# A first attention with 48-row scores: two 32-bit parts, alternating row halves, scores issued beside transposed scores

## What is computed

```python
# x: (4, 256, 256); 16 heads of 16 columns
q = _split(lora_linear(x, Wq, bq, Bq, Aq))       # k and v likewise
scores = jnp.einsum('bhqd,bhkd->bhqk', q, k) * SCALE
attn = jax.nn.softmax(scores, axis=-1)
out = jnp.einsum('bhqk,bhkd->bhqd', attn, v)
return lora_linear(out, Wo, bo, Bo, Ao)          # added to x by the caller
# feed-forward block: s = 1 / mean(|w|) of each of three weight matrices
```

## Time and the profile before

| | us |
|---|---|
| median of 3 runs | 788.89 (788.40 to 789.37) |
| the profiled execution | 788.12, span 786.3, mean granted clock 0.941 |
| first attention, from the start to its last residual | 0 to 109.4 |
| its loop on PE | 48.39 to 87.14 |
| its tail on PE | 87.14 to about 108 |
| loop of the cross-attention on PE | some 600 to 650 |

### The profile page before, as it was taken

How to read it: one execution, slowest core, us unless ns; L and a number is a source line. 1 busy time by engine, 2 the same in 40 slices (tenths; PEclk the granted TensorE clock), 3 DMA queues, 4 the chain that set the end, 5 groups by cost and what they waited for, 6 DMA issues and landing times. The chain is left out here.

```text
span 786.3 us, 13300 instructions
## 1 busy us (share of the span) xinstructions
PE 689.4 (88%) x4778; PEld 449.3 (57%) x4778; DVE 561.0 (71%) x1085; ACT 432.5 (55%) x896; POOL 196.8 (25%) x296
## 2 busy tenths in 40 slices
PE   5999989999999999999847469999868888889997
PEld 3555567566666756666433244666623444368886
DVE  5578678686868768686669973566568999475665
ACT  4557743635536373553649666455356999633222
POOL 2413001303032130303224514131022111352450
PEclk9999998999999999999978789999957999959999
DMA  4725432212112120210132205230020334403201
GB/s 124 190 66 163 132 102 61 75 23 66 47 43 51 52 76 19 71 45 7 28 119 33 75 8 148 79 99 3 2 61 6 72 82 106 120 2 109 78 29 54
DMA packets 55698, 53.59 MB, mean 68 GB/s; under 512 B 15526, under 2 KB 46310, under 8 KB 55526
## 3 DMA queue, kind: packets, MB, share of 16 engines
q1 hardware_dynamic: 54718, 52.27, 24.4%
q10 hardware_dynamic: 916, 0.47, 0.2%
HBM read 26.84 MB, written 2.04 MB: 37 GB/s over the span
## 5 line engine op out<-in xcount | busy, mean ns | idle before, releaser
L427 DVE TENSOR_REDUCE a_nm<-ps 128x2 f32<-128x512 f32 (+1 forms) x112 | 75.3, 688 | 28.2 <-PE ps L723 19.4
L2511 DVE TENSOR_REDUCE x_nm<-ps 128x2 f32<-128x512 f32 x128 | 80.0, 684 | 14.0 <-PE ps L2658 11.0
L1533 PE MATMUL ps<-m_xp,m_mp 128*128 128x512 f32 x288 | 77.4, 406 | 0.2 <-DVE m_wr L1236 0.2
L2594 ACT ACTIVATE x_pt<-ps 128x1024 f32<-128x1024 f32 x64 | 63.9, 1023 | 7.6 <-PE ps L2689 7.4
L1408 ACT ACTIVATE m_junk<-ps,m_nm 128x256 bf16<-128x256 f32 x128 | 58.6, 484 | 12.5 <-DVE m_nm L1253 12.5
L1200 POOL TENSOR_SCALAR fw<-fw,finv 128x256 f32<-128x256 f32 x24 | 11.6, 482 | 212.5 <-PE ps L1612 212.5
L2658 PE MATMUL ps<-kx,a_qs 48*128 48x256 bf16 x256 | 44.9, 297 | 19.3 <-DVE x_nm L2511 11.4
L1533 PEld LDWEIGHTS ps<-m_xp,m_mp 128*128 128x128 f32 x288 | 52.2, 193 | 14.7 <-issue 4.8
L3110 PE MATMUL ps<-x_xp,x_wp 128*128 128x512 f32 x216 | 54.8, 405 | 0.0
L1216 DVE TENSOR_TENSOR m_qcs<-ps,mw_tab 64x512 f32<-64x512 f32 x64 | 44.1, 688 | 7.6 <-PE ps L1533 6.1
L1223 DVE TENSOR_TENSOR m_qcs<-ps,mw_tab 128x512 f32<-128x512 f32 x64 | 41.2, 685 | 7.5 <-PE ps L1533 7.2
(11 more groups left out here) (304 smaller groups left out, 1660.3 us busy)
## 6 DMA issues: line engine op xcount, KB each, us to landing
a_qs<-a_parts SPq DMA_DIRECT2D x48, 128.0 KB
a_ks<-a_parts SPq DMA_DIRECT2D x48, 128.0 KB
m_q<-m_qs SPq DMA_DIRECT2D x32, 128.0 KB
x_gb<-scr_g SPq DMA_DIRECT2D x8, 512.0 KB, 3.7
fw<-in_f_w SPq DMA_DIRECT2D x12, 256.0 KB
a_qs<-a_ks SPq DMA_DIRECT2D x46, 64.0 KB
mw_wq<-in_m_wq SPq DMA_DIRECT2D x8, 256.0 KB, 2.9
mw_wo<-in_m_wo SPq DMA_DIRECT2D x8, 256.0 KB, 2.9
```

The source lines that it names most:

```text
L427: dve.tensor_reduce(dst, src, AX.X, ALU.max, negate=True).then_inc(mx_done.sem, 1)
L1533: mm = pe.matmul(c.ps[:, QB_BANKS[k], :], mp[:, p % 2, w, dt, tile * P:(tile + 1) * P], xp[:, x, dt, half_cols(half)], start=((dt, w, x) = ...
L2511: dve.tensor_reduce(nm[:, n % ITEMS, QT * u:QT * u + QT], c.ps[:, score_bank(n, u), :].rearrange("p (t k) -> p t k", t=QT), AX.X, ALU.max, ...
L2594: act.activation(pt[:, n % 2, kt, :], c.ps[:, 2 + 2 * kt:4 + 2 * kt, :].rearrange("p b n -> p (b n)"), ACT.Exp, scale=SCALE).then_inc(exp_ ...
```

## The change

The first attention gets a function of its own, `first_attention`; the second keeps `attention_block`, and the rest of the program is the same.

- q and k are split into two 32-bit parts (`F32R`): ACT writes the high part, DVE the remainder, which is the second part. Three products of parts make 48 rows (50 with the maxima). Items 0 to 3 and 8 to 11 lie on partitions 0 to 49, items 4 to 7 and 12 to 15 on 64 to 113. POOL's low part and ACT's middle part are gone.
- SP sends six transfers of 256 KB for each of k = 0 and 1. For k = 2 and 3 each batch is sent apart, in six of 128 KB: the first batch early, the second when its slot has come free (`later_in`, waited for by `scores(10, 0)` and `scores(14, 0)`).
- The loop runs 11 times over `side_by_side` four times, `product` twice and `max_transpose`; LAG is 5 instead of 4, TLAG 4 instead of 3, and from item 5 on the scores have three banks. The tail has five products and four transposed scores instead of four and three. `outputs(n)` of the loop moves from DVE to ACT.
- The twelve weight loads are issued before the first send, and ACT's twelve sums stand between the parts in the head; the first of them waits for all twelve loads.
- POOL clears a second stretch of 32 partitions, and the first send waits for both.

```diff
+def first_attention(c, wqk_in, wvo, bias_io, first, scales, last_loads):
...
+    Q_TERMS, K_TERMS = (0, 0, 1), (0, 1, 0)
+    S_ROWS = len(Q_TERMS) * HD
+    T_ROWS = S_ROWS + 2
+    BASES = (0, 64)
...
+    LAG, TLAG = 5, 4
...
+    ORDER = ((0, 0), (0, 1), (1, 1), (1, 0))
...
+        parts = sb("parts", [P, 2, DT, 2, TOK], F32R)
...
+        def rows_of(tiles, n, first_row, last_row):
+            base = BASES[n // 4 % 2]
+            return by_slot(tiles, slice(base + first_row, base + last_row), slot(n))[:, n % 2, :, :]
...
+        def score_bank(n, u):
+            i = UNITS * n + u
+            return i % 2 if n < LAG else (0, 1, 7)[(i - UNITS * LAG) % 3]
...
+                def send_term(k, w, part, term, b):
+                    half, ot = ORDER[k]
+                    base = BASES[k % 2]
+                    rows = slice(base + term, base + S_ROWS, len(Q_TERMS))
+                    if k < 2:
+                        sp.dma_start((qr, kr)[w][0][rows], parts[:, w, ot, part, half_cols(half)].bitcast(F32))\
+                            .then_inc(part_in[k].sem, 16)
+                    else:
+                        q0 = half * BANK + b * SEQ
+                        sp.dma_start(by_slot((qr, kr)[w], rows, (2, 0)[b]), parts[:, w, ot, part, q0:q0 + SEQ].bitcast(F32))\
+                            .then_inc((later_in[k] if b else part_in[k]).sem, 16)
...
+                scales.loads(sp)
+                sp.wait_ge(cleared.sem, cleared.at(2))
+                send_all(0)
+                send_all(1)
+                send_all(2)
+                send_all(3)
+                max_rows_in(4)
+                sp.wait_ge(st_done.sem, st_done.at(2 * 2))
+                send(2, 0, 0, 1)
+                send(2, 1, 0, 1)
+                max_rows_in(5)
+                send(2, 0, 1, 1)
+                send(2, 1, 1, 1)
+                for n in range(6, 9):
+                    max_rows_in(n)
+                sp.wait_ge(st_done.sem, st_done.at(2 * 6))
+                max_rows_in(9)
+                send(3, 0, 0, 1)
+                max_rows_in(10)
+                send(3, 1, 0, 1)
+                max_rows_in(11)
+                send(3, 0, 1, 1)
+                send(3, 1, 1, 1)
+                for n in range(12, N):
+                    max_rows_in(n)
+                last_loads(sp)
...
+                for base in BASES:
+                    pool.memset(c.kflat[base + 32:base + 64, :].bitcast(F32), 1.0).then_inc(cleared.sem, 1)
+                pool.wait_ge(cleared.sem, cleared.at(2))
...
+                def remainder(g):
+                    w, ot, half = parts_of(g)
+                    dve.wait_ge(hi_done.sem, hi_done.at(g + 1))
+                    dve.scalar_tensor_tensor(parts[:, w, ot, 1, half_cols(half)], c.ps[:, 2 + g % 4, :],
+                                             bcol[:, w, ot:ot + 1], parts[:, w, ot, 0, half_cols(half)].bitcast(F32),
+                                             ALU.add, ALU.subtract).then_inc(lo_done.sem, 1)
...
+                def outputs(n):
+                    act.wait_ge(av_done.sem, av_done.at(n + 1))
+                    act.activation(outputs_of(place(n)[0])[:, place(n)[1], :], c.ps[:, 6, 0:SEQ], ACT.Copy)\
+                        .then_inc(out_done.sem, 1)
...
+                high(2)
+                sums(0, 1)
+                high(3)
+                sums(1, 5)
+                high(4)
+                sums(5, 7)
+                high(5)
+                sums(7, 8)
+                high(6)
+                sums(8, 9)
+                high(7)
+                sums(9, 11)
+                values(0)
+                sums(11, 12)
...
+                for n in range(N - LAG):
+                    exponentials(n + 1, 0)
+                    exponentials(n + 1, 1)
+                    max_rows(n + TLAG)
+                    outputs(n)
...
+                def may_score(n, u):
+                    if u == 0 and n % 4 == 0:
+                        pe.wait_ge(part_in[n // 4].sem, part_in[n // 4].at(16 * 6))
+                    if u == 0 and n in (10, 14):
+                        pe.wait_ge(later_in[n // 4].sem, later_in[n // 4].at(16 * 6))
+                    i = UNITS * n + u
+                    if i == UNITS * LAG + 2:
+                        pe.wait_ge(mt_done.sem, mt_done.at(TLAG))
+                    elif i > UNITS * LAG + 2:
+                        pe.wait_ge(mx_done.sem, mx_done.at(i - 2))
+                    elif i > 1:
...
+                def side_by_side(n, u, n_t, kt, h):
+                    may_score(n, u)
+                    if h == 0:
+                        may_score_t(n_t, kt)
+                    score(n, u, 0)
+                    score_t(n_t, kt, h)
+                    score(n, u, 1).then_inc(s_done.sem, 1)
+                    mm = score_t(n_t, kt, h + 1)
...
+                project(4)
+                scores(0, 0, 1)
+                project(5)
+                scores(0, 2)
+                project(6)
+                scores(0, 3)
+                project(7)
+                scores(1, 0)
+                project_bias()
+                scores(1, 1)
+                project_values(0)
+                scores(1, 2)
...
+                scores(3, 0, 1)
+                project_values(7)
+                scores(3, 2, 3)
+                scores_t(0, 0)
+                scores_t(0, 1)
+                max_transpose(2)
+                scores(4, 0, 1, 2, 3)
+                max_transpose(3)
+                for n in range(N - LAG):
+                    side_by_side(n + LAG, 0, n + 1, 0, 0)
+                    side_by_side(n + LAG, 1, n + 1, 0, 2)
+                    side_by_side(n + LAG, 2, n + 1, 1, 0)
+                    side_by_side(n + LAG, 3, n + 1, 1, 2)
+                    product(n, 0)
+                    product(n, 1)
+                    max_transpose(n + TLAG)
...
+                scores_t(N - 4, 0)
+                max_transpose(N - 1)
+                product(N - 5, 0)
+                turn_outputs(0)
+                product(N - 5, 1)
+                scores_t(N - 4, 1)
+                turn_quotients(0)
+                turn_outputs(1)
+                scores_t(N - 3, 0)
+                product(N - 4, 0)
+                output_project(0)
+                turn_quotients(1)
+                product(N - 4, 1)
+                scores_t(N - 3, 1)
+                turn_outputs(2)
+                output_project(1)
...
-    def loads(self, sp, j):
-        if j >= 4:
-            sp.wait_ge(self.summed.sem, j - 3)
-        sp.dma_start(self.part(j), self.c.io["f_w"][j // 4, :, j % 4 * BANK:(j % 4 + 1) * BANK])\
-            .then_inc(self.w_in[j % 4].sem, 16)
+    def loads(self, sp):
+        for j in range(self.CHUNKS):
+            sp.dma_start(self.part(j), self.c.io["f_w"][j // 4, :, j % 4 * BANK:(j % 4 + 1) * BANK])\
+                .then_inc(self.w_in.sem, 16)
...
     def scalar(self, act, j):
-        act.wait_ge(self.w_in[j % 4].sem, self.w_in[j % 4].at(16 * (j // 4 + 1)))
+        if j == 0:
+            act.wait_ge(self.w_in.sem, self.w_in.at(16 * self.CHUNKS))
```

More of the change, by code:

```diff
@@ L969, in __init__ @@
         self.ones = st.enter_context(c.nc.sbuf_tensor("fs_ones", [P, P], F32))
-        self.w_in = [c.counter(f"at_in{4 + k}") for k in range(4)]
+        self.w_in = c.counter("at_in4")
         self.summed, self.total, self.scales = c.counter("fw_sum"), c.counter("fw_total"), c.counter("fw_step")
@@ L3177, in build_program @@
             first, scales = FirstLoads(c, st), WeightScales(c, st)
-            attention_block(c, st, "a0", first.raw, first.wvo, "L0_bias", first=first, scales=scales, last_loads=c.mla.first)
+            first_attention(c, first.raw, first.wvo, "L0_bias", first, scales, c.mla.first)
             first.const_in.done(48)
-            for w in scales.w_in:
-                w.done(16 * 3)
+            scales.w_in.done(16 * scales.CHUNKS)
         mla_stage(c)
```

529 lines of the change are left out of this document (added).

## The result

| | before | after |
|---|---|---|
| median, us | 789.13 (788.40 to 793.04, 4 runs) | 811.31 (809.56 to 815.68, 4 runs) |
| profiled execution, us | 788.12, span 786.3 | 810.13, span 807.7 |

The change makes the kernel slower: ratio 1.029, 95% interval 1.0264 to 1.0316. The direction was forecast, the size was not: +22 us instead of +3.6, far outside the range. I take the two traces apart by starts of the same PE instructions.

What follows compares the result with a forecast made beforehand. PE was taken to bound head, loop and tail, with a dependency chain closing the new loop. Terms 1.9 + 0.5 - 4.5 + 1.6 + 4.1 = +3.6 on 788.12 gave 791.7 us; whole range 785.0 to 796.0.

Steps and rivals of the forecast that it cites:

- Mode changes in the head: Head: each of twelve score places between projections costs 0.62 us with its mode changes; head +1.9 us.
- The pass of the loop: Loop: a pass takes 2.82 us instead of 3.23, over eleven passes -4.5 us.
- the chain: Loop: dependent steps from an item's first maximum to the next item's, not one engine, set the pass: 2.60 plus 0.22 us.
- the rival of no overlap in 32 bits: Loop: the row halves don't overlap, a pass takes 3.3 us, time 797.0 us; chance 0.08.
- that of the hidden changes: All stages: cold starts and mode changes going in vanish, 5.5 us less, time 786.2 us; chance 0.28.
- The wait before item 14: Loop: `scores(14, 0)` waits for the late second batch of k = 3, +1.6 us, bounds 0 and 2.7.
- The tail: Tail: one item more, cold starts and mode changes, +4.1 us, bounds +2.3 and +4.8.
- The weights at the head: Head: twelve weight loads queue ahead of the first sends, +0.5 us, bounds 0 and +2.5.
- the weights come too late: Head: rival with 2.5 us instead of 0.5 for late weights, time 793.7 us; chance 0.07.
- the forecast's sign: Whole kernel: the change makes it slower, +3.6 us; chance of slower 0.55.
- the +1.5 of the prediction's terms: Head +1.9, loop -4.5 and tail +4.1 us, without the waits for copies.

Runs made afterwards that it cites:

- e10: Against the change: one clear, row halves alternating by batch, first batch of k = 0 sent first, only k = 3 late; 794.45 us, ratio 1.0070 to before.
- e11: e10 with head scores in pairs between projections, 7 places instead of 12; 795.75 us, ratio 1.0090 to before.
- e6: The change with one memset of all 128 rows of the key tile instead of two of 32; 805.5 us, single run.
- e4: The change with the sends for the second batch of k = 3 ahead of the rows of maxima of items 9 and 10; 803.4 us, single run.
- e12: e11 with the sends of k = 2 held until the first transposed scores are done; 793.06 us, ratio 1.0048 to before.
- e13: e10 with an unused extra product of 1.06 us in PE's gap ahead of the loop; 796.52 us, ratio 1.0102 to before.
- e8: The change with the sums of absolute weights moved from the head back into the loop, loads still at the head; 815.4 us, single run.

## Why the prediction was wrong, step by step

- **Mode changes in the head: right.** A place of one unit takes 47.60 - 47.17 = 0.43, and the next unit follows 1.06 later instead of 0.86 (33.38 to 34.24 before, below): 0.63, predicted 0.62. Without late copies (e10) the last values end near 49.3 (49.2) and the loop starts at 54.0 (53.4), and e11's fewer places give back 1.76.

```profile
33.38 1.03 PE L694 MATMUL ps<-lora_wvo,a_bvb 128*128 128x256 f32 x4
34.24 0.39 PE L710 MATMUL ps<-a_ks,a_qs 96*128 96x256 bf16 x2
```

- **The pass of the loop: right.** 2.81 against 2.82, with PE waiting for DVE once in a pass, and the second matmul of a group 0.22 behind its start (77.98, 78.20). It was no luck: from the first maximum (78.52) the links of the chain measure 0.74 to the fourth score (79.26), 0.44 to the products (79.70), 1.09 to the next item's first score (80.79), 0.22 to its second half and 0.32 to the next maximum, against 0.75, 0.32 + 0.10, 1.10, 0.11 + 0.10 and 0.32. Scores and transposed scores of the two halves start together (77.98 and 77.99), so the rival of no overlap in 32 bits falls; that of the hidden changes falls by the 0.63 of a place and the 0.22 of a start.
- **The wait before item 14: right mechanism, mis-sized.** 2.64 against 1.6, at the upper bound of 2.7. The mis-sized term is the landing, 2.6 because "idle queues can be quicker": the last send was issued at 91.01, 2.0 behind the transpose of item 11 as predicted, and waited for until 94.72, 3.7 later, as in the earlier trace rows.

```profile
91.01 0.60 SPq L313 DMA_DIRECT2D a_ks<-a_parts  x1
```

- **The tail: right direction, a little short.** Up to the last transposes of outputs (104.18 before, 124.14 after) 21.95 instead of 17.04 us, +4.9 against +4.1, just beyond the bound of +4.8. Of this 0.55 is a wait for DVE at 124.14 that before does not have; the other parts were not tested apart.
- **"The weights at the head": this step failed.** The weights were no trouble: they ran at 384 GB/s, not 278, and the DMA share falls to 0.26 from 18.6 on. The step then took "1.57 MB for k = 0 at 203 GB/s" and a share of 0.75 to mean that full engines would copy in proportion faster, 271 GB/s or 5.8 us, and land it by 28.1. But the 203 of the earlier trace rows were of copies to rows spread over 96; the copies to 48 rows fill the DMA engines at 125. They were also issued 1.8 us later, because POOL's second clear held DVE up (e6), where the step called it free; the row of SP's queue that answers to 18.61 in the earlier trace rows is

```profile
20.39 1.27 SPq L309 DMA_DIRECT2D a_qs<-a_parts  x2
```

  The DMA share rises to 1.06 at about 22; from there 1.57 MB at 125 GB/s (12.6 us) last until 34.6, and the score started at 35.12. The term of +0.5 (bound 2.5) measured 6.5 as the wait alone, and `project(4)` came 0.9 later, of which e6's single clear gives 0.8 back.
- **A term that was missing: the granted clock.** Every wait was priced at its own length, and the loop's start at full clock. Worked out from rows: from 35.1 to 38.5 at half clock, half of it lost, 1.7; the passes of 4.36 and 3.11 behind item 14, 1.9; and at the loop's start, behind no wait for a copy of parts, two passes of 4.36 and one of 3.11 from 63.3, 3.4 more than three of 2.81. Together 7.0 us in this one execution; in e4, which changes nothing before item 9, only one pass at the loop's start is slow.

The sum closes to 0.2 us: the prediction missed 6.0 (wait beyond its term), 0.9, 1.7 and a rest of 0.8 in the head, 1.0 + 3.4 + 1.9 in the loop, and 0.9 in the tail; 16.6, and with +3.6 the 20.0 found. The rest of 0.8 is not explained in full; 0.36 of it is a wait for a row of maxima before 59.33. The rival "the weights come too late" had the right place and the wrong cause and price. What e10 shows beside this is that the forecast's sign did not hang on the copies: without them the saving of the loop is smaller than what head and tail pay. Its +4.6 against the +1.5 of the prediction's terms is 0.5 more in the head, 1.7 in the loop (most of it half clock at its start) and 0.9 in the tail.

Still open: why the clock falls at the start of the loop even in e10, e12 and e13, and how long it stays down; and why steps of 3 copy at 126 GB/s and not faster. Matmuls on half of the rows alone do not keep it down, since the later passes run at 1.00, and short idle time alone need not bring it down: in the kernel before PE stood idle for 0.80, 0.57 and 0.21 us ahead of its loop (45.07, 47.11, 47.70), and the clock stayed at 1.00.

## What to carry to other kernels

Price a copy between on-chip rows by the rate that its own destination rows allow when the DMA engines are full, not by the rate that another copy showed while its issue set the pace (128 KB every 0.64 us is 205 GB/s, the 203 of the earlier trace rows). Price a wait of PE with the half clock that can follow it, as a range: here waits of 6.5 and 2.6 us cost 1.7 and 1.9 more, and behind the 5.2 of e8 10 us ran at half clock, some 5 lost. A stage elsewhere in the same trace that already has the new form is the best source for a loop's pass: with the longer 32-bit starts added it was right to 0.01 us.

## What the runs showed of the hardware that was not expected

- The rate of copies at a full DMA share goes by the destination rows: 111 GB/s (16 rows in a block), 126 (steps of 3), 205 (steps of 4), and 156 to 161 with steps of 3 in alternating halves.
- POOL's memsets held a DVE instruction of 0.17 us for 3.95 us.
- The time of a memset did not go by its rows: two of 32 rows took 10.48 us, one of all 128 rows in e6 5.22, and one of 32 rows in before 5.21.
- A small transfer that PE needs (a row of maxima) waits for large copies that are under way, though it is issued on another engine's queue: PE stood 1.21 us for it in e11, and not at all in e12, which holds the copies back.
